# A message-passing kernel whose TensorE stages each lag the stage they need by one full step

## The chip, the core and the metric

The kernel runs on one core of a Trainium2 chip. The metric is device time in microseconds (us) of the whole program. The core's engines are TensorE (PE for its matmuls, PEld for its weight loads), VectorE (DVE), ScalarE (ACT), GpSimd (POOL) and SyncE (SP, which only issues DMAs here); they run at the same time and wait for one another through semaphores.

## The reference

A graph layer: 200,000 edges, sorted by their target node, over 12,500 nodes with 32 features each. Each edge goes through four dense layers, the results are averaged by target node, added to the node's features and normalised.

```python
x_j = x[j_idx]                       # source row
x_i = x[i_idx]                       # target row
msg = jnp.concatenate([x_i, x_j - x_i], axis=-1)   # 64
h = jax.nn.relu(msg @ W1 + b1)       # 64
h = jax.nn.relu(h @ W2 + b2)         # 128
h = jax.nn.relu(h @ W3 + b3)         # 64
m = h @ W4 + b4                      # 32
s = jax.ops.segment_sum(m, i_idx, num_segments=N_NODES)
cnt = jax.ops.segment_sum(jnp.ones((m.shape[0],), m.dtype), i_idx, num_segments=N_NODES)
...
x = _layernorm(x + s / jnp.maximum(cnt, 1.0)[:, None], axis=-1)
```

## The kernel before

**Steps.** The edges are worked on in 196 steps of 1,024 edges, two halves (h) of 512 each. Because the edges are sorted by target, a step touches only a narrow window of nodes, so the target's part of layer 1 and the sum by target are matmuls against small 0/1 matrices that VectorE builds (`build_pick`, L1259, L1260, L1262; `build_onehot`, L1301). The source rows come in one of two ways:

- **gathered steps** (138): GpSimd fetches rows already multiplied by W1 with 8 indirect DMAs of 128 rows each (L564) into a ring of ten steps, and TensorE turns them into layer 1's PSUM bank (`turn_rows`, L859). A slot of the ring is free again when its step has been turned, which is what GpSimd waits for.
- **sorted steps** (58): the edges of the step were sorted by source beforehand, and TensorE picks the rows by 113 small bf16 matmuls against one-hots (`selected_x`, L897). VectorE builds these one-hots in 8 chunks (`build_hot`, L1270) from index rows that SyncE spreads over all partitions (L467, 366 to 407 KB each); there are five buffers for them. ScalarE (L664) and VectorE (L1280) copy the picked rows to SBUF, and `selected_layer1` (L911) multiplies them by W1.

From step 14 on every third step is a sorted one, up to step 185: a **period** is one sorted and two gathered steps, and there are 58 of them. The first ten steps (AHEAD) run beside a sort on VectorE. Five of them are "plain": their rows are not yet multiplied by W1 (L872).

**Stages of a step.** Layer 1 with the target's part (`add_dst`, L841) → ReLU on ScalarE (L675) → layer 2 (L921) → ReLU (two halves, L683) → layer 3 (L929) → ReLU (L690) → turned (L937) → copied by VectorE (L1289) → summed by target window (L952, sorted steps L949) → added to the sums by VectorE (L1316). Each of the stages on TensorE has one PSUM buffer; the SBUF buffers between them are double.

**Order.** Every engine has an order written out by hand: a function `step(s)` per engine names what is done in round s, and for which step. TensorE's is, before the change: rows of s (for a sorted step all 113 matmuls), turn of s-2, window sum of s-3, the sorted step's layer 1, layer 3 of s-1, layer 2 of s. So layer 2 of s follows layer 1 of s in the same round, and layer 3 of s-1 stands one round after its layer 2. VectorE in round s builds chunks 5 to 7 of its one-hots if s is sorted, copies the rows, copies the turned layer 3 of s-2, builds the pick of s+1 and the one-hot of s-2, adds the sums of s-3, and builds chunks 0 to 4 for sorted steps ahead. An engine waits at its next instruction and everything behind it waits too.

## Time and profile before

| what | us |
|---|---|
| median of 3 runs | 2545.24 (2544.97 to 2545.98) |
| the profiled execution | 2551.01 |
| its span, first to last instruction | 2549.2 |
| TensorE matmul busy | 1782.1 (70%) |
| TensorE weight loads busy | 1173.7 (46%) |
| GpSimd busy | 1093.8 (43%) |
| VectorE busy | 844.8 (33%) |
| ScalarE busy | 634.2 (25%) |

The granted clock of TensorE over the span is 0.803 of full speed; it has two levels, 1.2 and 2.4 GHz. The table gives averages over a front part with a sort and few matmuls (to about 415 us), the 58 periods (to about 2415 us), a row of gathered steps and the last layer. In the profile a matmul's start is recorded and its end is modelled; when its result was really there is seen at the instruction of another engine that waited for it. "remote" as what ended a wait means that the profile finds no instruction whose recorded end fits it.

### The profile page before, as it was taken

The numbers are of one execution on the slowest core, as the hardware profiler recorded it, in microseconds if no ns is written. First come the engines' busy times: TensorE is split into PE (matmuls) and PEld (weight loads), VectorE is DVE, ScalarE is ACT, GpSimd is POOL, SyncE is SP. The second block draws the span as 40 slices with busy tenths as digits, with TensorE's granted clock in tenths as the row PEclk, the third lists the DMA queues.
The fourth block names the chain that finished last, engine by engine and source line by source line (L and its number), as shares of the span: only waits on it lengthen the run. The fifth ranks groups of instructions, "written<-read, shape, count | busy, mean of one in ns | idle before, by whom it ended". The sixth has DMA issues, their size and how long they took to land.

```text
span 2549.2 us, 39560 instructions
## 1 busy us (share of the span) xinstructions
PE 1782.1 (70%) x13928; PEld 1173.7 (46%) x13928; DVE 844.8 (33%) x1777; ACT 634.2 (25%) x999; POOL 1093.8 (43%) x1123
## 2 busy tenths in 40 slices
PE   2133516777787777787777777777877778777887
PEld 2111303555454554555554555554555545555547
DVE  2342602333333333333333333332333333333352
ACT  2222314222222222222222222222222222222241
POOL 4175263444444444444444444444344444444402
PEclk9975756878878788878888878888788888887885
DMA  3221414444434444444444444443444443444310
GB/s 114 81 65 29 114 35 149 142 133 133 132 112 140 137 139 125 126 123 142 139 138 125 127 123 142 136 138 105 128 142 137 139 123 120 131 142 133 93 58 27
DMA packets 194466, 300.61 MB, mean 118 GB/s; under 512 B 83633, under 2 KB 90015, under 8 KB 193697
## 3 DMA queue, kind: packets, MB, share of 16 engines
q1 hardware_dynamic: 158439, 260.74, 32.3%
q0 software_dynamic: 35168, 35.43, 6.7%
q8 instruction: 116, 1.90, 0.3%
q10 hardware_dynamic: 658, 1.85, 0.2%
q14 instruction: 85, 0.70, 0.1%
HBM read 283.89 MB, written 13.87 MB: 117 GB/s over the span
## 4 chain that ended last, share of the span: by engine, by line
PE 41%; another core or an unknown queue 22%; issue 16%; DVE 9%; DMA 5%; ACT 3%; DVEq 3%; SPq 0%; POOL 0%; ACTq 0%; POOLq 0%
PE ps L897 21%; PE ps L921 5%; PE ps L929 3%; PE ps L949 3%; DVEq L1314 3%; PE ps L937 2%; PE ps L841 2%; PE ps L911 2%; PE ps L998 2%; DVE region L1270 2%; DVE region L1301 2%; PE ps L859 1%; DMA dstb<-dst_rows 1%; DMA y_rows<-work 1%
## 5 line engine op out<-in xcount | busy, mean ns | idle before, releaser
L564 POOL DMA_INDIRECT xj<-z_rows,src_t x1059 | 1038.2, 980 | 1293.4 <-PE ps L859 785.6
L897 PE MATMUL ps<-region,x_p 128*96 128x155 bf16 (+51 forms) x6554 | 611.4, 259 | 268.5 <-issue 238.0
L897 PEld LDWEIGHTS ps<-region,x_p 128*96 128x96 bf16 x6554 | 544.1, 162 | 395.4 <-issue 367.3
L1270 DVE TENSOR_SCALAR region<-region,cst 128x1629 bf16<-128x1629 int16 x464 | 274.0, 643 | 348.6 <-remote 295.1
L929 PE MATMUL ps<-work,w3s 128*64 128x512 f32 x784 | 311.5, 697 | 69.0 <-ACT work L683 38.5
L683 ACT ACTIVATE work<-ps,b2s 128x512 f32<-128x512 f32 x392 | 256.8, 685 | 205.7 <-remote 147.0
L1289 DVE COPY work<-ps 128x512 f32<-128x512 f32 x188 | 129.2, 687 | 504.0 <-remote 278.5
L921 PE MATMUL ps<-work,w2s 64*128 64x512 f32 x784 | 252.9, 726 | 45.5 <-ACT work L675 41.1
L690 ACT ACTIVATE work<-ps,b3s 128x512 f32<-128x512 f32 x196 | 134.7, 687 | 529.6 <-remote 468.4
L675 ACT ACTIVATE work<-ps,b1s 128x512 f32<-128x512 f32 x196 | 134.8, 688 | 507.7 <-PE ps L841 363.0
L937 PE MATMUL ps<-cst,work 128*128 128x128 f32 x784 | 138.3, 303 | 139.8 <-ACT work L690 99.3
L1316 DVE TENSOR_TENSOR sums<-sums,ps 65x42 f32 (+1 forms) x334 | 67.7, 203 | 361.3 <-remote 179.0
L952 PE MATMUL ps<-region,work 128*65 128x42 f32 x2208 | 177.3, 248 | 12.4 <-issue 6.6
L952 PEld LDWEIGHTS ps<-region,work 128*65 128x65 f32 x2208 | 175.8, 159 | 12.9 <-issue 11.5
L921 PEld LDWEIGHTS ps<-work,w2s 64*128 64x128 f32 x784 | 65.4, 204 | 237.0 <-ACT work L675 164.8
L937 PEld LDWEIGHTS ps<-cst,work 128*128 128x128 f32 x784 | 89.7, 150 | 178.0 <-ACT work L690 112.4
L664 ACT ACTIVATE work<-ps 96x512 bf16<-96x512 f32 x58 | 34.4, 593 | 491.5 <-PE ps L897 491.5
L929 PEld LDWEIGHTS ps<-work,w3s 128*64 128x64 f32 x784 | 61.4, 150 | 150.4 <-ACT work L683 84.4
L1280 DVE CAST work<-ps 96x512 bf16<-96x512 f32 x58 | 39.8, 687 | 247.5 <-PE ps L897 247.5
L859 PEld LDWEIGHTS ps<-cst,xj 128*128 128x128 f32 x552 | 59.8, 144 | 127.5 <-issue 127.5
L859 PE MATMUL ps<-cst,xj 128*128 128x128 f32 x552 | 93.6, 294 | 20.5 <-DVE work L1233 19.3
L841 PE MATMUL ps<-region,ywin 126*64 126x512 bf16 x508 | 93.1, 400 | 20.8 <-DVE region L1262 11.6
(156 smaller groups left out, 940.2 us busy)
## 6 DMA issues: line engine op xcount, KB each, us to landing
dstb<-dst_rows SPq DMA_DIRECT2D x196, 252.0 KB
region<-src_rows SPq DMA_DIRECT2D x116, 391.2 KB
region<-src_rows SPq DMA_DIRECT2D x58, 407.2 KB
region<-src_rows SPq DMA_DIRECT2D x58, 403.2 KB, 4.8
region<-src_rows SPq DMA_DIRECT2D x58, 376.2 KB
region<-src_rows SPq DMA_DIRECT2D x58, 375.8 KB, 3.7
region<-src_rows SPq DMA_DIRECT2D x58, 374.0 KB
region<-src_rows SPq DMA_DIRECT2D x58, 366.2 KB, 5.4
```

Source lines behind the costliest of these rows:

```text
L564: pool.indirect_dma_start(out=xj[:, u, j % UT, j // UT, 0:w], out_offset=None, in_=rows, in_offset=bass.IndirectOffsetOnAxis(ap=cols[:, j: ...
L675: nc.scalar.activation(h1[:, v, :], p_h1, ACT.Relu, bias=b1s[:, 0:1]).then_inc(s_r1, 1)
L683: nc.scalar.activation(h2[:, v, h, :], p_h2[:, h, :], ACT.Relu, bias=b2s[:, 0:1]).then_inc(s_r2[h], 1)
L690: nc.scalar.activation(h3[:, v, :], p_h3, ACT.Relu, bias=b3s[:, 0:1]).then_inc(s_r3, 1)
L841: added = nc.tensor.matmul(p_h1[h * H1:(h + 1) * H1, :], rows, pick[:, v, k, h * UE:(h + 1) * UE], start=False, stop=k == steps - 1, skip_ ...
L859: turned = nc.tensor.matmul(to[:, t * T:(t + 1) * T], xj[:, u, t, :, :].rearrange("p h f -> p (h f)"), ident, start=t == 0, stop=True, is_ ...
L897: chosen = nc.tensor.matmul(ps[0:XP, XBANK[h], lo - h * UE:hi - h * UE], xb[:, a, :], hot[:, q % QN, at + lo:at + hi], start=not begun[h], ...
L921: nc.tensor.matmul(p_h2[:, h, :], w2s[r:r + H1, :], h1[r:r + H1, s % 2, :], start=True, stop=True).then_inc(s_l2[h], 1)
L929: nc.tensor.matmul(p_h3[h * H3:(h + 1) * H3, :], w3s[:, :], h2[:, s % 2, h, :], start=True, stop=True).then_inc(s_l3, 1)
L937: turned = nc.tensor.transpose(p_ht[:, t * T:(t + 1) * T], h3[:, s % 2, t * T:(t + 1) * T], ident)
L952: summed = nc.tensor.matmul(p_agg[:, h * KN:(h + 1) * KN], h3t[:, v, t, h, :], onehot[:, v, j, 0:KN], start=t == 0, stop=t == UT - 1)
L1270: nc.vector.tensor_scalar(hot[:, q % QN, 0:CW[c]], spread[:, q % QE, 0:CW[c]], cst[:, C_PID:C_PID + 1], None, ALU.is_equal).then_inc(s_hot, 1)
```

## The change

TensorE's round s becomes: layer 1 of s (for a sorted step it needs the rows already picked), then **the picking of rows for s+1 if that one is sorted**, layer 2 of s-1, layer 3 of s-2, turn of s-3, window sum of s-4. Each stage now needs what was done a full round earlier. ScalarE and VectorE follow in the same manner: the ReLUs of a round come in the order 1, 2, 3 for s, s-1, s-2; the copies of the picked rows are for s+1; VectorE first adds the sums of s-5, and the one-hot chunks come a step earlier than before (chunks 0 and 1 three steps ahead, 2 to 4 two, 5 to 7 one). The first sorted step is 15 instead of 14, so one more gathered step stands ahead of the periods and one fewer behind them, and each engine has one round more to empty the pipeline. SyncE's loads of index rows move a round earlier as well. GpSimd's code is untouched.

```diff
-FIRST_SORTED, PERIOD = AHEAD + 4, 3
+FIRST_SORTED, PERIOD = AHEAD + 5, 3
...
             def step(s):
-                if is_sorted(s) and STEPS[s] + 1 < SB:
+                if s + 1 < S_N and is_sorted(s + 1) and STEPS[s + 1] + 1 < SB:
                     for c in range(CN - QN):
-                        load_windows(STEPS[s] + 1, QN + c)
+                        load_windows(STEPS[s + 1] + 1, QN + c)
                 if s + RX < S_N:
                     load_dst(s + RX)
                     load_rows(s + RX)
...
-                if s + 1 < S_N and is_sorted(s + 1) and STEPS[s + 1] + 1 < SB:
+                if s + 2 < S_N and is_sorted(s + 2) and STEPS[s + 2] + 1 < SB:
                     for c in range(QN):
-                        load_windows(STEPS[s + 1] + 1, c)
+                        load_windows(STEPS[s + 2] + 1, c)
...
             def step(s):
-                if s >= 1:
-                    relu2(s - 1)
-                if s < S_N and is_sorted(s):
-                    copy_x(s)
                 if s < S_N:
                     relu1(s)
-                if 2 <= s < AHEAD:
-                    copy_layer3(s - 2)
-                if s >= 1:
-                    relu3(s - 1)
+                if s + 1 < S_N and is_sorted(s + 1):
+                    copy_x(s + 1)
+                if 1 <= s <= S_N:
+                    relu2(s - 1)
+                if 2 <= s <= S_N + 1:
+                    relu3(s - 2)
+                if 3 <= s < AHEAD:
+                    copy_layer3(s - 3)
...
             def step(s):
+
                 if s < S_N:
                     if is_sorted(s):
-                        selected_x(s)
+                        selected_layer1(s)
                     elif is_plain(s):
                         plain_x(s)
                     else:
                         gathered_x(s)
+                if s + 1 < S_N and is_sorted(s + 1):
+                    selected_x(s + 1)
+                if 1 <= s <= S_N:
+                    layer2(s - 1)
                 if 2 <= s <= S_N + 1:
-                    turn_layer3(s - 2)
-                if s >= 3:
-                    sum_window(s - 3)
-                if s < S_N and is_sorted(s):
-                    selected_layer1(s)
-                if 1 <= s <= S_N:
-                    layer3(s - 1)
-                if s < S_N:
-                    layer2(s)
+                    layer3(s - 2)
+                if 3 <= s <= S_N + 2:
+                    turn_layer3(s - 3)
+                if s >= 4:
+                    sum_window(s - 4)
...
             def step(s):
-                if s < S_N and is_sorted(s):
+                if s >= 5:
+                    add_sums(s - 5)
+                if s + 1 < S_N and is_sorted(s + 1):
                     for c in range(QN, CN):
-                        build_hot(STEPS[s], c)
-                if s < S_N and (is_sorted(s) or is_plain(s)):
+                        build_hot(STEPS[s + 1], c)
+                    copy_x(s + 1)
+                if s < S_N and is_plain(s):
                     copy_x(s)
-                if AHEAD <= s <= S_N + 1:
-                    copy_layer3(s - 2)
                 if s + 1 < S_N:
                     build_pick(s + 1)
-                if 2 <= s <= S_N + 1:
-                    build_onehot(s - 2)
-                if s >= 3:
-                    add_sums(s - 3)
-                for lead, some in ((2, (0, 1)), (1, (2, 3, 4))):
+                if AHEAD <= s <= S_N + 2:
+                    copy_layer3(s - 3)
+                if 3 <= s <= S_N + 2:
+                    build_onehot(s - 3)
+                for lead, some in ((3, (0, 1)), (2, (2, 3, 4))):
```

The order on TensorE, before, from the second gathered step of a period to the first matmuls that pick the sorted step's rows (L897), with the semaphores each row waits for (`relu2_unit0` and `relu2_unit1` are ScalarE's two halves):

```order
L859 MATMUL ps<-cst,xj 128x128 [waits gathered1,relu1]
L859 MATMUL ps<-cst,xj 128x128 x3
L841 MATMUL ps<-region,ywin 64x512 [waits pick_built,window_in1]
L841 MATMUL ps<-region,ywin 64x512
L937 MATMUL ps<-cst,work 128x128 [waits layer3_copied,relu3]
L937 MATMUL ps<-cst,work 128x128 x3
L952 MATMUL ps<-region,work 65x42 [waits sums_added,onehot_built,layer3_copied]
L952 MATMUL ps<-region,work 65x42 x7
L929 MATMUL ps<-work,w3s 64x512 [waits relu2_unit0,relu3]
L929 MATMUL ps<-work,w3s 64x512 [waits relu2_unit1]
L921 MATMUL ps<-work,w2s 128x512 [waits relu2_unit0,relu1]
L921 MATMUL ps<-work,w2s 128x512 [waits relu2_unit1]
```

And now, in the same place; a line number of the changed kernel is that of before plus one here:

```order
L860 MATMUL ps<-cst,xj 128x128 [waits gathered4,relu1]
L860 MATMUL ps<-cst,xj 128x128 x3
L842 MATMUL ps<-region,ywin 64x512 [waits pick_built,window_in2]
L842 MATMUL ps<-region,ywin 64x512
L898 MATMUL ps<-region,x_p 96x26 [waits source_onehots,x_copied_unit1,x_copied_unit0]
...
L898 MATMUL ps<-region,x_p 96x20
L922 MATMUL ps<-work,w2s 128x512 [waits relu2_unit0,relu1]
L922 MATMUL ps<-work,w2s 128x512 [waits relu2_unit1]
L930 MATMUL ps<-work,w3s 64x512 [waits relu2_unit0,relu3]
L930 MATMUL ps<-work,w3s 64x512 [waits relu2_unit1]
```

The picking (all its rows lie at the "...") moved from behind the whole second gathered step to right behind its layer 1; the four stages that stood ahead of it now follow it, and they are of older steps.

On VectorE, before, the round of a sorted step: chunks 5 to 7 of the one-hots (`chunks_selected` tells that TensorE is done with an older chunk) stand ahead of the copies and the pick.

```order
L1270 TENSOR_SCALAR region<-region,cst 128x1503
L1270 TENSOR_SCALAR region<-region,cst 128x1613
L1270 TENSOR_SCALAR region<-region,cst 128x1465
L1280 CAST work<-ps 96x512
L1289 COPY work<-ps 128x8x64
L1262 TENSOR_SCALAR region<-dstb,node_off 126x1024
L1301 TENSOR_TENSOR region<-iota_g,dst_rel 128x8x42
```

Now this stands in the round of the gathered step ahead of it, behind that round's sums:

```order
L1318 TENSOR_TENSOR sums<-sums,ps 65x84
L1272 TENSOR_SCALAR region<-region,cst 128x1503
L1272 TENSOR_SCALAR region<-region,cst 128x1613
L1272 TENSOR_SCALAR region<-region,cst 128x1465
L1282 CAST work<-ps 96x512
L1261 TENSOR_SCALAR region<-dstb,node_off 126x1024
L1262 TENSOR_SCALAR region<-dstb,node_off 126x1024
L1291 COPY work<-ps 128x8x64
```

The sums moved to the head of the round, and the copy of the turned layer 3 moved behind the pick.

## Rows read from the trace of the kernel before

**Rows 1.** The page: part 1 (busy, share); of part 5 one group (busy, mean | idle before).

```profile
PE 1782.1 (70%) x13928; PEld 1173.7 (46%) x13928; DVE 844.8 (33%) x1777; ACT 634.2 (25%) x999; POOL 1093.8 (43%) x1123
...
L897 PE MATMUL ps<-region,x_p 128*96 128x155 bf16 (+51 forms) x6554 | 611.4, 259 | 268.5 <-issue 238.0
```

**Rows 2.** Table by stretch: front part with two gather stretches, then the periods.

```profile
core 0: us, PE busy (x) PEld busy (x) DVE busy (x) ACT busy (x) POOL busy (x), PEclk, DMA share, GB/s
...
130.00:243.00 113.00, 30.23 (x88) 11.75 (x88) 39.34 (x93) 21.96 (x22) 79.89 (x79) 0.63 0.23 50
...
302.00:381.00 79.00, 17.52 (x81) 9.32 (x79) 5.71 (x11) 16.46 (x46) 53.20 (x56) 0.54 0.19 41
...
415.00:2415.00 2000.00, 1551.00 (x12590) 1024.63 (x12591) 669.50 (x1382) 485.02 (x742) 888.91 (x907) 0.82 0.44 132
```

**Rows 3.** Timeline of TensorE in a gathered step while GpSimd is idle.

```profile
2424.69 0.66 PE L859 MATMUL ps<-cst,xj 128*128 128x128 f32 x4
...
2425.61 0.66 PE L937 MATMUL ps<-cst,work 128*128 128x128 f32 x4
...
2429.19 0.66 PE L859 MATMUL ps<-cst,xj 128*128 128x128 f32 x4
```

**Rows 4.** Table by stretch of one period, in its order; the last is another block.

```profile
1515.16:1519.66 4.50, 4.50 (x36) 2.48 (x35) 1.50 (x3) 1.85 (x3) 2.84 (x3) 1.00 0.34 87
1519.66:1530.68 11.02, 8.55 (x36) 3.27 (x34) 3.93 (x8) 2.75 (x4) 7.38 (x8) 0.69 0.25 48
1530.68:1539.32 8.64, 3.84 (x45) 3.07 (x44) 2.21 (x5) 1.84 (x3) 5.46 (x6) 0.89 0.84 250
1539.32:1545.36 6.04, 6.04 (x70) 6.04 (x71) 1.67 (x3) 0.59 (x1) 0.00 (x0) 0.59 0.70 214
1545.36:1550.30 4.94, 4.94 (x43) 2.72 (x41) 2.34 (x5) 1.38 (x2) 0.00 (x0) 1.00 0.18 47
...
2407.70:2415.27 7.57, 6.70 (x116) 6.38 (x114) 4.17 (x9) 2.44 (x4) 1.58 (x2) 1.00 0.24 51
```

**Rows 5.** Timeline of TensorE in the two gathered steps of that period.

```profile
1517.59 1.08 PE L929 MATMUL ps<-work,w3s 128*64 128x512 f32 x4
...
1519.66 0.66 PE L859 MATMUL ps<-cst,xj 128*128 128x128 f32 x4
...
1522.56 0.66 PE L937 MATMUL ps<-cst,work 128*128 128x128 f32 x4 [1.91 <-ACT work L690]
...
1524.31 1.97 PE L929 MATMUL ps<-work,w3s 128*64 128x512 f32 x2
1526.84 1.97 PE L929 MATMUL ps<-work,w3s 128*64 128x512 f32 x2 [0.56 <-ACT work L683]
1528.74 2.02 PE L921 MATMUL ps<-work,w2s 64*128 64x512 f32 x4
```

**Rows 6.** Timeline of GpSimd: first gather of a period, ninth, sixteenth, next period's first.

```profile
1516.09 0.94 POOL L564 DMA_INDIRECT xj<-z_rows,src_t  x1 [14.12 <-PE ps L859]
...
1527.77 0.95 POOL L564 DMA_INDIRECT xj<-z_rows,src_t  x1 [1.64 <-remote]
...
1536.73 0.94 POOL L564 DMA_INDIRECT xj<-z_rows,src_t  x1 [0.30 <-issue]
1551.20 0.95 POOL L564 DMA_INDIRECT xj<-z_rows,src_t  x1 [13.53 <-PE ps L859]
```

**Rows 7.** Timelines of ScalarE and VectorE: instructions that waited for TensorE's results.

```profile
1521.82 0.69 ACT L690 ACTIVATE work<-ps,b3s 128x512 f32<-128x512 f32 x1 [4.72 <-remote]
...
1526.10 0.69 ACT L683 ACTIVATE work<-ps,b2s 128x512 f32<-128x512 f32 x1 [2.14 <-remote]
```

**Rows 8.** Timeline of TensorE: the picking of rows while GpSimd gathers.

```profile
1530.68 1.75 PE L897 MATMUL ps<-region,x_p 128*96 128x26 bf16 x29
1533.10 0.75 PE L897 MATMUL ps<-region,x_p 128*96 128x146 bf16 x5 [0.66 <-DVE region L1270]
```

**Rows 9.** Waits of the front part (130 to 415 us): in total, times, longest.

```profile
ACT work L690 <- remote: 45.9, 3, 27.4
```

More of the change, by code:

```diff
@@ L357, in layer3_copied @@
         def layer3_copied(eng, s):
-            if s < AHEAD - 2:
+            if s < AHEAD - 3:
                 eng.wait_ge(s_h3a, s + 1)
             else:
-                eng.wait_ge(s_h3c, s + 3 - AHEAD)
+                eng.wait_ge(s_h3c, s + 4 - AHEAD)
         def piece(h):
@@ L726, in _ @@
                     nc.scalar.activation(src16[:, :], scr0.bitcast(I32), ACT.Copy).then_inc(s_cast, 1)
+            act.wait_ge(s_cast, 2)
             act.wait_ge(s_end, 1)
@@ L729, in _ @@
             with act.Fori(0, end, WIN) as off:
-                for s in range(AHEAD, S_N + 1):
+                for s in range(AHEAD, S_N + 2):
                     step(s)
-                    if AHEAD <= s < SSTEP[0] - 1:
+                    if AHEAD <= s < SSTEP[0] - 2:
                         for c in range(3 * (s - AHEAD), min(3 * (s - AHEAD) + 3, CN)):
@@ L986, in _ @@
             with pe.Fori(0, end, WIN) as off:
-                for s in range(AHEAD, S_N + 3):
+                for s in range(AHEAD, S_N + 4):
                     step(s)
@@ L1369, in _ @@
                 mask_sorted()
-                for s in range(AHEAD, S_N + 3):
+                for s in range(AHEAD, S_N + 5):
                     step(s)
```

6 lines of the change are left out of this document (3 added, 3 removed).

## Prediction, made before the changed kernel ran

> **What bounds the kernel now.** I read the share of each engine first. TensorE's matmuls are busy 70% of the span and GpSimd's gathers 43% [rows 1], so TensorE is the bound, with 30% in which it stands. The table by stretch says where the time lies: 2,000 of the 2,549 us are the 58 periods; the front part has two long stretches, 113 and 79 us, in which TensorE has only 88 and 81 matmul records [rows 2].
>
> Next, a step that nothing disturbs. With GpSimd idle a gathered step takes 2429.19 - 2424.69 = 4.50 us, one group of matmuls right behind the other, no wait [rows 3]. There the old order hides every round trip already: a deeper pipeline could give nothing.
>
> Then one period by its stages [rows 4]: first gathered step 4.50, second gathered step 11.02, picking of rows 8.64 + 6.04, rest of the sorted step 4.94; together 35.1 us. The second gathered step and the picking are the slow ones: undisturbed they take 4.50 [rows 3] and 7.57, the last row of [rows 4]. What the slow parts share is GpSimd: its 16 gathers run from 1516.09 to 1537.67, with one pause of 1.64 us, and it is idle until 1551.20 [rows 6]. Inside that stretch two things are seen.
>
> First, TensorE's results are told late. The first gathered step's layer 3 is issued at 1517.59 and should be done a us later, yet its ReLU on ScalarE starts at 1521.82, after 4.72 us without an instruction; a half of layer 2's ReLU starts 1526.10, for a layer 2 that stands ahead of the turn at 1519.66 [rows 5, 7]. So a round trip costs 3 to 7 us instead of one. TensorE then waits itself: 1.91 us for the ReLU of layer 3, and layer 3's halves, which ran side by side in 1.08 us a step earlier, are issued 2.53 us apart and take 1.97 us each, at the lower clock (granted mean 0.69) [rows 4, 5].
>
> Second, small instructions crawl although nothing they wait for is missing. Picking starts with 29 matmuls in 1.75 us [rows 8]; up to 1539.32 there are 43 (the 45 records of that stretch less two of the layer 2 ahead), so the last 14 take 1539.32 - 1533.10 = 6.2 us, 2.3 a us; behind it come 70 in 6.04 us, 11.6 a us [rows 4]. The end of the crawl is 1.65 us behind the last gather's end.
>
> **The change part by part.** No matmul, DMA, copy or activation of a period is added or removed; it is a matter of order.
>
> (a) *Second gathered step.* Its layer 1 (L859, L841) takes 0.92 us, turn, sum, layer 3 and layer 2 the other 3.58 [rows 3]. All four now need what was done a round earlier, so the round trips of 3 to 7 us lie under a round of 4.5. The parts of the two gathered steps that stay inside the gather stretch are 3.58 + 0.92 = 4.5 us of work instead of 15.5 - 0.9 = 14.6 us of time. Gain at most 14.6 - 4.5 = 10.1 us, of which 3.58 is only moved behind the picking.
>
> (b) *Picking moves into the crawl.* It begins about 4.5 to 5.5 us into the gather stretch instead of 14.6, so about 9 us more of it meet the crawl. TensorE's period, counted from the first gather, is then: end of the crawl at 1539.32 - 1516.09 = 23.2; what is left of the 113 matmuls at 0.086 us each (6.04 / 70); 3.58 for the four stages behind them; 4.94 for the sorted step; 0.9 to the turn that frees GpSimd. That is 32.6 + 0.086 x (113 - k), k being the matmuls issued by the end of the crawl. The old order fits the same sum: 23.2 + 6.04 + 4.94 + 0.9 = 35.1. For k: at the crawl's slow rate 43 + 9 x 2.3 = 64, period 36.8; all 113, period 32.6; at the mean rate of the old 8.64 us (5.0 a us) 43 + 9 x 5.0 = 88, period 34.8. I take 88: the picking now also has the early, livelier part of the stretch and GpSimd's pause, where the old order had only the end. Gain 0.3 us x 58 = 17 us.
>
> (c) *VectorE and ScalarE.* VectorE's work of a period (11.7 us by its rows [rows 4]) is the same. Chunks 5 to 7 of the one-hots now wait for TensorE a round earlier, with the copy of the picked rows, the two picks and the copy of layer 3 queued behind; who needs them is the next round's layer 1 and turn, 3.58 us of TensorE's work later. The picks and copies take about 2.4 us, so this is hidden; if that cover goes, it costs up to 1 us a period. ScalarE's copy of the picked half stands ahead of the ReLU of layer 2, whose matmul comes behind the picking anyway: nothing. SyncE's index rows move a round earlier, and the loads of target rows three steps ahead are queued behind them as before: nothing. GpSimd's gathers are freed by the same turn.
>
> (d) *Front part.* In the two gather stretches TensorE issues a matmul each 113 / 88 = 1.3 us and 79 / 81 = 1.0 us [rows 2], and one ReLU of layer 3 waits 27.4 us [rows 9]. The new order puts off layer 2, layer 3, turn and sum of a step by a round: about 20 to 28 records that lie ahead of the next rows in the crawl and are later paid at 4.5 us a step. Ends: a gain of 28 x 1.3 - 4.5 = 32 us, or no gain (below zero too: a loss of 5, if GpSimd's gathers are freed sooner and the crawl lasts longer). I take 20, since VectorE, too, no longer waits for sums of s-3 but of s-5.
>
> (e) *End.* One more round to empty the pipeline, one gathered step fewer behind the periods; the same matmuls. Between 0 and one step of 4.5 us; I take 2.
>
> Sum against the profiled execution: 2551.0 - 17 - 20 + 2 = 2516; the median of the runs shown is 5.8 us below that execution, so 2510.
>
> **A rule that speaks against my reading.** The rows show matmuls slow while GpSimd gathers and fast once it stops [rows 4, 6, 8]. The Trainium skill, "SBUF — State Buffer", section "SBUF: two separate sides", says that TensorE's SBUF port never waits for anyone and that only VectorE and GpSimd share a port. By it the gathers would cost TensorE nothing; the trace so far speaks against it, and the rival built on it is the last one below.
>
> **Rivals.**
>
> *Slower: the picking crawls all the way.* It decides from k: 35.1 = 32.6 + 0.086 x (113 - k) gives k = 84, that is 4.6 matmuls a us over the added 9 us; with the front's gain of 20 us (0.34 a period) the even point is k = 80. At 2.3 a us the period is 36.8: +1.7 x 58 = +99, with -20 and +2 about 2626. For it: 14 matmuls in 6.2 us are the only direct sample of that rate, and in the front part, where gathers run without a pause for longer, the rate is 1 a us. Now nothing stops GpSimd for 1.64 us if the second turn is told sooner. Against it: 29 matmuls went through at full pace, and the change gives TensorE the stretch's beginning.
>
> *Much faster: nothing of the picking is left when the gathers end.* k = 113, period 32.6: -2.5 x 58 = -145, with -20 about 2382. For it: 17.7 us are there for work that takes 7.57 undisturbed. Against it: chunk 5's one-hots need the first chunk reported as done, and this is just what comes late.
>
> *No change.* The stretch lets a fixed amount of work through whatever its order, and the front gains nothing: 2545. For it: the stretch's end hangs on GpSimd alone in both orders.
>
> *GpSimd disturbs nothing; the slow parts are round trips only.* Then the period falls to 4.5 + 4.5 + 7.6 to 10 + 4.9, about 22.5 us, still over GpSimd's 16 gathers, (1537.67 - 1516.09 - 1.64) = 19.9 us [rows 6]: -12.6 x 58, about 1800. Against it: 238.0 of the 268.5 us that TensorE idles ahead of the picking's matmuls end with no wait at all [rows 1].
>
> **How the numbers follow.** Forecast as summed, 0.40, with a range of its own of 2470 to 2535; slower 0.33; much faster 0.12; no change 0.12; the last rival 0.03. A range that leaves out no more than two in ten reaches from the much faster case to most of the slower one: 2380 to 2612. What a measurement of this kernel can tell from no change is about 0.2%, 5 us. Faster: 0.40 + 0.12 + 0.03 = 0.55; same 0.12; slower 0.33.
>
> **What would show each step right or wrong.** (a): in the gather stretch, no wait of layers 2 and 3 or of the turn for ScalarE; two gathered steps' worth of work ahead of the picking in about 5 us. (b): count the picking's matmuls between its start and the end of the crawl, and the period from one first gather to the next: below 35.1 or above. (c): a wait of layer 1 of the sorted step for a pick or a copied half would be new. (d): the periods begin at about 415 us [rows 2], and one gathered step more stands ahead of them now; a first picking that starts ahead of 415 shows the gain. The prediction falls if the picking's rate in the stretch is below 4 a us, or if GpSimd's pause, and so the stretch, becomes longer.

## The result, and the profile after

The changed kernel took 2684.82 us (median of 4 runs, 2681.97 to 2688.92), the kernel before beside it 2545.17 (4 runs): a ratio of 1.0549, 95% interval 1.0531 to 1.0568. It is 5.5% slower. The forecast was 2510 with a range of 2380 to 2612, so both the sign and the range were wrong. The profiled execution spans 2683.2 us.

The page of the changed kernel, shares of the engines and the groups that answer to [rows 1]. Line numbers of TensorE's code are higher by one now (picking is L898), those of VectorE by two:

```profile
PE 1691.2 (63%) x13928; PEld 1144.3 (43%) x13928; DVE 839.3 (31%) x1778; ACT 613.6 (23%) x998; POOL 1090.5 (41%) x1123
...
L898 PE MATMUL ps<-region,x_p 128*96 128x155 bf16 (+51 forms) x6554 | 677.1, 259 | 678.9 <-issue 678.6
...
L1272 DVE TENSOR_SCALAR region<-region,cst 128x1629 bf16<-128x1629 int16 x464 | 275.7, 637 | 896.9 <-remote 827.8
...
L930 PE MATMUL ps<-work,w3s 128*64 128x512 f32 x784 | 215.5, 627 | 0.5 <-ACT work L690 0.5
```

TensorE is busy for 63% instead of 70%. Its idle time ahead of picking matmuls rose from 268.5 to 678.9 us, nearly all of it "issue": time in which it waited for nothing that the profile shows. Its waits for ScalarE's ReLUs are gone: 0.5 us ahead of layer 3 in the whole span. In the kernel before they were 38.5 us there, 41.1 ahead of layer 2 and 99.3 ahead of the turn, the largest (total, times, longest):

```profile
PE ps L937 <- ACT work L690: 99.3, 39, 15.1
```

So the lag did what it says, and the time is lost elsewhere.

Where it is lost, from the timeline of TensorE in the changed kernel: the start of the first picking, of the second and of the last.

```profile
405.30 1.50 PE L898 MATMUL ps<-region,x_p 128*96 128x26 bf16 x15
...
435.13 0.80 PE L898 MATMUL ps<-region,x_p 128*96 128x26 bf16 x13
...
2536.39 1.31 PE L898 MATMUL ps<-region,x_p 128*96 128x26 bf16 x22
```

In the kernel before these stood at 414.92, 446.65 and 2407.70. The part up to the second picking is 11.5 us shorter; the 56 periods behind it take (2536.39 - 435.13) / 56 = 37.52 us instead of 35.02, which is +140 us; the rest of the span, 146.8 us instead of 141.5, is +5.3. The three make +134, the difference of the two spans.

One period of the changed kernel, in its order, as [rows 4] shows one of before: the work between the first gather and the picking, the early part of the picking, its crawl, its rest, and all up to the next period's first gather.

```profile
core 0: us, PE busy (x) PEld busy (x) DVE busy (x) ACT busy (x) POOL busy (x), PEclk, DMA share, GB/s
...
1593.06:1597.65 4.59, 4.59 (x37) 2.62 (x35) 3.47 (x9) 2.53 (x4) 3.67 (x4) 1.00 0.26 59
1597.65:1600.37 2.72, 1.68 (x30) 1.56 (x28) 1.24 (x3) 0.00 (x0) 2.11 (x3) 1.00 0.74 220
1600.37:1616.07 15.70, 4.24 (x28) 2.99 (x27) 0.62 (x1) 0.69 (x1) 9.91 (x11) 0.60 0.43 133
1616.07:1621.51 5.44, 5.44 (x61) 5.42 (x61) 1.15 (x2) 0.59 (x1) 0.00 (x0) 0.59 0.49 187
1621.51:1630.60 9.09, 9.09 (x73) 4.78 (x73) 5.03 (x11) 4.37 (x7) 0.00 (x0) 1.00 0.22 65
```

Work goes at full pace for 4.59 us of gathers, then the picking puts through 27 matmuls and crawls for 15.70 us, in which only 27 more are issued: 1.7 a us. The crawl's inside, from the timeline of TensorE:

```profile
1597.65 1.69 PE L898 MATMUL ps<-region,x_p 128*96 128x26 bf16 x27
1600.37 0.29 PE L898 MATMUL ps<-region,x_p 128*96 128x143 bf16 x2 [1.04 <-issue]
1601.12 0.23 PE L898 MATMUL ps<-region,x_p 128*96 128x146 bf16 x1 [0.46 <-issue]
...
1611.79 0.44 PE L898 MATMUL ps<-region,x_p 128*96 128x124 bf16 x3 [2.37 <-issue]
1614.62 0.38 PE L898 MATMUL ps<-region,x_p 128*96 128x44 bf16 x3 [2.39 <-issue]
1615.36 0.31 PE L898 MATMUL ps<-region,x_p 128*96 128x93 bf16 x1 [0.35 <-issue]
1616.07 5.44 PE L898 MATMUL ps<-region,x_p 128*96 128x65 bf16 x59 [0.40 <-issue]
```

Matmuls come out one to four at a time, with 0.30 to 2.39 us between, and each gap is "issue". GpSimd's timeline, as in [rows 6]: first gather of the period, ninth, sixteenth, the next period's first.

```profile
1593.06 1.21 POOL L564 DMA_INDIRECT xj<-z_rows,src_t  x1 [17.28 <-PE ps L860]
...
1603.57 0.94 POOL L564 DMA_INDIRECT xj<-z_rows,src_t  x1 [0.30 <-issue]
...
1612.30 1.03 POOL L564 DMA_INDIRECT xj<-z_rows,src_t  x1 [0.30 <-issue]
1630.60 1.21 POOL L564 DMA_INDIRECT xj<-z_rows,src_t  x1 [17.27 <-PE ps L860]
```

The pause of 1.64 us ahead of the ninth gather [rows 6] is gone. That holds for the whole trace: in the kernel before the break lasts 1.2 to 2.05 us in every period, here it is the 0.30 us that lie between any two gathers. The sixteen run in one unbroken row, most starts 1.25 us apart (mean 1.28), and the crawl ends 2.7 us behind the last of them. The clock adds to it. TensorE stands for most of the crawl (4.24 us busy of 15.70), its granted clock falls to a mean of 0.60, and the 59 matmuls behind take 5.44 us at a mean of 0.59: the lower of its two levels, 0.50, up to 1620.0, the upper one at the end; a whole picking of 113 takes 6.4 us at full clock (below).

### The profile page after: what moved, and what is told of

Read it like the earlier page. It is cut to its first block, busy times and chain, and to the rows that moved or that the text cites. A ratio compares the mean times of both kernels' runs of the same rounds, so it can differ in the third digit from the quotient of the medians.

```text
span 2683.2 us, 39558 instructions
## 1 busy us (share of the span) xinstructions
PE 1691.2 (63%) x13928; PEld 1144.3 (43%) x13928; DVE 839.3 (31%) x1778; ACT 613.6 (23%) x998; POOL 1090.5 (41%) x1123
## 3 DMA queue, kind: packets, MB, share of 16 engines
q0 software_dynamic: 35168, 35.43, 6.3%
## 4 chain that ended last, share of the span: by engine, by line
PE 57%; issue 26%; DMA 1%; DVE 1%; DVEq 0%; POOL 0%; SPq 0%; ACT 0%; POOLq 0%
PE ps L898 25%; PE ps L922 7%; PE ps L930 7%; PE ps L953 4%; PE ps L938 4%; PE ps L950 3%; PE ps L842 2%; PE ps L860 2%; PE ps L912 2%; PE ps L1000 2%; DMA region<-in_x 1%; DVEq L1316 0%; DMA src_rows<-region 0%; DMA region<-src_rows 0%; POOL region L596 0%
## 5 line engine op out<-in xcount | busy, mean ns | idle before, releaser
L898 PE MATMUL ps<-region,x_p 128*96 128x155 bf16 (+51 forms) x6554 | 677.1, 259 | 678.9 <-issue 678.6
L898 PEld LDWEIGHTS ps<-region,x_p 128*96 128x96 bf16 x6554 | 570.2, 159 | 793.8 <-issue 790.2
L1272 DVE TENSOR_SCALAR region<-region,cst 128x1629 bf16<-128x1629 int16 x464 | 275.7, 637 | 896.9 <-remote 827.8
L683 ACT ACTIVATE work<-ps,b2s 128x512 f32<-128x512 f32 x392 | 248.5, 684 | 316.4 <-PE ps L922 287.3
L922 PE MATMUL ps<-work,w2s 64*128 64x512 f32 x784 | 234.2, 670 | 6.2 <-issue 6.2
L930 PE MATMUL ps<-work,w3s 128*64 128x512 f32 x784 | 215.5, 627 | 0.5 <-ACT work L690 0.5
L953 PE MATMUL ps<-region,work 128*65 128x42 f32 x2208 | 155.8, 233 | 74.5 <-DVE sums L1318 38.8
L953 PEld LDWEIGHTS ps<-region,work 128*65 128x65 f32 x2208 | 152.8, 143 | 75.6 <-issue 74.4
L938 PE MATMUL ps<-cst,work 128*128 128x128 f32 x784 | 129.6, 287 | 2.1 <-issue 2.0
L930 PEld LDWEIGHTS ps<-work,w3s 128*64 128x64 f32 x784 | 39.6, 136 | 156.6 <-issue 154.7
L950 PE MATMUL ps<-region,work 128*65 128x84 f32 x928 | 77.9, 238 | 7.7 <-DVE sums L1318 7.7
```

Of the source, the lines that this page charges most:

```text
L683: nc.scalar.activation(h2[:, v, h, :], p_h2[:, h, :], ACT.Relu, bias=b2s[:, 0:1]).then_inc(s_r2[h], 1)
L898: chosen = nc.tensor.matmul(ps[0:XP, XBANK[h], lo - h * UE:hi - h * UE], xb[:, a, :], hot[:, q % QN, at + lo:at + hi], start=not begun[h], ...
L922: nc.tensor.matmul(p_h2[:, h, :], w2s[r:r + H1, :], h1[r:r + H1, s % 2, :], start=True, stop=True).then_inc(s_l2[h], 1)
L930: nc.tensor.matmul(p_h3[h * H3:(h + 1) * H3, :], w3s[:, :], h2[:, s % 2, h, :], start=True, stop=True).then_inc(s_l3, 1)
L938: turned = nc.tensor.transpose(p_ht[:, t * T:(t + 1) * T], h3[:, s % 2, t * T:(t + 1) * T], ident)
L950: summed = nc.tensor.matmul(p_agg, h3t[:, v, t, h, :], onehot[:, v, j, :], start=j == 0, stop=j == PT - 1)
```

## The experiments

The eighteen runs fell on six chips, A to F. The kernel before ran on each, and **it finds two kinds of chip**. On A, C and D it took 2546.8, 2570.0 and 2559.4 us, much as on the chip of the result; on B, E and F 1608.8, 1611.1 and 1613.7 us. I call them the first and the second kind; nothing in a program chooses one. Each chip was used for one short time only, so whether the kind belongs to the chip for good or to its state at the time is not shown. Each run is told against the kernel before on its own chip; on A to D each time is that of a single run. Periods are mean distances between the starts of pickings, the second to the last, as above.

**One gather instead of eight, old order and new** (chip A, first kind; before 2546.8 us). The other rows of each step are left out of the computation; the sums are those of wrong rows.

```
 def gathers_of(g):
+    if g >= AHEAD + 5:
+        return 1
     return PT if g < GB - 1 else LAST
```

> The kernel before with 1 of the 8 row gathers of each gathered step from the 16th gathered step on (the other rows stay stale; sums are those of wrong rows). Theory D (GpSimd's gathers make TensorE's small instructions crawl and its results late): the period falls from 35.0 us to about 4.5 + 4.5 + 7.6 to 10 + 4.9 = 22 to 24 us, total about 2545 - 57 x 12 = 1860. Theory R (the slow parts of the period are round trips and waits of TensorE, ScalarE and VectorE among themselves): nothing changes, 2540. Theory L (the loads of index rows, 3.1 MB a period, make it crawl): nothing changes, 2540.

> The changed kernel with the same gathers left out. Theory D: 22 to 24 us a period as in the kernel before, within 1 us of it, total 1840 to 1880; what the new order costs is gone. Theory W (the new order has a wait of its own, for one-hot chunks or index rows that now come too late): still 2.5 us a period slower than the kernel before without gathers, about 140 us in all.

Measured: 1661.13 us for the old order, 1644.87 for the new, periods of 20.24 and 20.14 us. That is theory D in kind, and some 200 us below its numbers, which had put the period at 22 to 24 us. The table by stretch of the new order with one gather, over 1,100 us of its periods:

```profile
360.00:1460.00 1100.00, 1100.00 (x11976) 757.11 (x11975) 612.74 (x1314) 447.91 (x711) 129.66 (x110) 1.00 0.62 205
```

TensorE is busy all the time at full clock. So 15 to 17 us of each period go with the gathers, in either order. Without them the new order is 16 us the faster, so it holds no wait of its own, and the index-row loads of SyncE, which are all still there, cost nothing by themselves. The change loses only where the gathers are; whether they need the loads beside them to do harm is not shown, since no run leaves the loads out.

**Gathers put behind the picking** (chip A).

```
 if g >= R:
     pool.wait_ge(s_turned, g - R + 1)
+if g >= AHEAD + 5:
+    picked = sum(1 for s in SSTEP if s < GSTEP[g - R]) + 1
+    if GSTEP[g - R] > SSTEP[0] and picked <= SB:
+        pool.wait_ge(s_block, CN * picked)
```

> The changed kernel with one wait more: in the periods GpSimd starts a step's gathers only when TensorE has finished the picking that follows (the chunks_selected semaphore). The 16 gathers (19.9 us) then start beside layers 2 and 3 of the second gathered step and lie on 13.9 us of large matmuls before they meet the next picking. Theory D: at most 6 us of gathers plus 2.7 us behind them fall on the picking; period about 29 us, total 2685 - 57 x 8 = about 2230, below both kernels. Theory W: no gain, 2685 or more; theory that GpSimd's gathers are needed early: a new wait of TensorE for gathered rows.

A miss, and the most useful one: 2683.2 us, period 37.46. The picking now runs at full pace, as no gather lies beside it, and what gets slow is the work that lies beside the gathers instead. TensorE's timeline in that kernel:

```profile
1505.56 1.01 PE L926 MATMUL ps<-work,w2s 64*128 64x512 f32 x1 [1.55 <-issue]
1507.66 1.01 PE L926 MATMUL ps<-work,w2s 64*128 64x512 f32 x1 [1.09 <-issue]
1510.48 1.86 PE L926 MATMUL ps<-work,w2s 64*128 64x512 f32 x2 [1.82 <-issue]
...
1519.14 6.45 PE L902 MATMUL ps<-region,x_p 128*96 128x26 bf16 x113
```

Layer 2, four matmuls in 1.13 us when nothing disturbs them, takes from 1505.56 to 1512.3 (the granted clock is 0.50 there). So the loss belongs to the row of gathers and not to the kind of work beside it: my picture of a picking that "crawls" and of larger steps that mostly wait for round trips was too narrow. A period of 37.5 us is not far from 20.1 us of work and 20 us of gathers one after the other, here and in the changed kernel.

**The lag alone, picking in its own round** (chip A). Of the diff, the later stages keep their full step of lag; the picking, its copies, one-hots and loads go back to the step that uses them.

```
 def step(s):
     if s < S_N:
         if is_sorted(s):
-            selected_layer1(s)
+            selected_x(s)
 ...
-    if s + 1 < S_N and is_sorted(s + 1):
-        selected_x(s + 1)
 ...
+    if s < S_N and is_sorted(s):
+        selected_layer1(s)
```

> The change without its second half: each stage lags by a full step, but the rows of a sorted step are picked in its own round, ahead of layer 2 of the step before, and layer 1 of the sorted step closes the round; first sorted step 14 as before. Theory D: the picking begins 3.6 us later in the gather stretch than in the changed kernel, so of the crawl at 1.7 matmuls a us it loses 6 matmuls (0.5 us) and gains 3.6 us of large matmuls: period 37.5 - 3.1 = 34.4, total about 2500. If the deeper lag itself costs: about 2685 as the changed kernel.

Measured: 2589.78 us, period 35.83, a miss too (2500 and 34.4 were expected). The lag alone costs 43 us, and the picking ahead of its step another 95 (against the 2684.82 us of the result's chip; the changed kernel as it is did not run on A): neither pays. In this kernel GpSimd still pauses for some 2 us between the eighth and the ninth gather of a period; with the picking ahead the pause is gone. That is the lead that the run with one pause follows, below. Why the lag alone makes the period 0.8 us longer than the 35.02 of before was not followed up.

**Room between the gathers** (chips B and C). Two theories were left. N: each gather costs about 1 us wherever it lies. B: what costs is the unbroken row, and gathers with room between them are free. Behind each gather from the sixteenth gathered step on, GpSimd writes a small tile of its own and waits for that write. Nothing is left out of the computation.

```
     pool.indirect_dma_start(out=xj[:, u, j % UT, j // UT, 0:w], ...)
         .then_inc(s_gath[u], 16)
+    if g >= AHEAD + 5:
+        nc.gpsimd.memset(pause[:, :], 0.0).then_inc(s_pause, 1)
+        paused[0] += 1
+        pool.wait_ge(s_pause, paused[0])
```

> The changed kernel, with a small write of GpSimd's own (one partition, 192 values) and a wait for it behind every gather from the sixteenth gathered step on: the gathers stay 16 a period, but their starts are some 1.7 to 1.9 us apart instead of 1.25. Theory B (what slows TensorE is the unbroken row of gathers, and single ones with room between cost nothing): the crawl goes or shrinks, the period falls from 37.5 to about 28 to 32 us (16 gathers then take 28 to 30), some 2150 to 2400 us. Theory N (each gather costs about 1 us wherever it lies; 20.2 us of work + 16 x 1.08): the period stays at 37.5 and the time within 1% of 2684.

> The same with 768 values in GpSimd's write, so that the gathers start some 2.2 to 2.6 us apart. Theory B: TensorE no longer waits for anything but the gathers themselves, 16 x 2.2 to 2.6 = 35 to 41 us a period, GpSimd busy throughout, the picking at its full pace of 6.4 us; 2550 to 2900 us. Theory N: the sum of both, the gathers' loss of 1.08 us each on 20.2 us of work while the gathers take 35 to 41, so the picking and the other steps still lose about 17 us a period; the time is then at least 2684.

> The changed kernel with 4 of the 8 gathers of each gathered step from the sixteenth on (the other rows keep what the buffer held: this part of the computation is left out), 8 a period instead of 16. Theory N (a loss for each gather): the period is 20.2 + 8 x 1.08 = 28.8 us, about 2190 us. Theory B (nothing below four or five gathers in a row, then a crawl): bursts of 4 with room between, a period of 20.2 to 22 us, 1640 to 1760 us; where the two bursts of 4 join to one of 8, about 24 us and 1900.

Chip B is of the second kind, with the kernel before at 1608.83 us. Short pause 1860.72 us (period 24.7), long pause 2315.97 us (32.3), four gathers of eight 1561.94 us (20.14). There was no crawl to take away, so these say nothing on what the crawl hangs on. They say what a pause costs: GpSimd becomes the bound.

> The changed kernel as it is, on whichever chip this call gets. The runs so far fell on two chips: on the first the kernel before took 2545 to 2547 us, on the second 1608.8, with all that the gathers cost on the first gone. On a chip of the first kind: 2684 us, 5.5% above before. On one of the second kind there is no crawl to lose by, and both theories leave TensorE as the bound: period 20.2 us as in the runs with one gather, so 1580 to 1600 us, 1 to 2% below before, from the hidden round trips alone.

> The kernel of e6_pause_short again. On a chip of the second kind 1861 us as there. On one of the first kind it tells what the first call was meant to: theory B (the unbroken row is what slows TensorE): with starts 1.54 us apart the crawl shrinks and the period falls to 25 to 32 us, 1900 to 2400 us; theory N (a loss of 1.08 us for each gather wherever it lies): the period stays at 37.5 us, some 2684.

> The changed kernel with one pause of some 1.5 to 2 us of GpSimd between the eight gathers that the first gathered step of a period releases and the eight of the second (a write of 1300 values on one partition and the wait for it). On a chip of the first kind: if the unbroken row of 16 is what the change costs in a period (37.5 against 35.0 us), the period falls to about 35 us, 2540 to 2560 us; if the break is worth nothing, 37.5 us and 2684; if the pause only adds, 38 to 39. On one of the second kind: the 16 gathers take 20 us of a period of 20.2, so the pause makes GpSimd the bound at about 22 us, 1680 to 1710 us.

Chip C is of the first kind, before at 2569.98 us. The changed kernel took 2679.41 us (period 37.51): slower again, here by 4.3%. With the short pause it took **1957.47 us**, 27% less, and 24% less than the kernel before, with the same gathers and the same work; period 25.6. GpSimd's timeline in it:

```profile
863.93 0.95 POOL L568 DMA_INDIRECT xj<-z_rows,src_t  x1 [0.27 <-issue]
864.88 0.25 POOL L572 MEMSET pause<- 1x192 f32 x1
865.40 0.95 POOL L568 DMA_INDIRECT xj<-z_rows,src_t  x1 [0.27 <-issue]
```

Starts are 1.47 us apart instead of 1.25 (a mean of 1.6, where some of the writes take longer), and 16 x 1.6 = 25.6 us is the period: the gathers' own time is the bound now. TensorE beside it, in one of the periods with a remnant of the crawl:

```profile
859.99 5.00 PE L906 MATMUL ps<-region,x_p 128*96 128x26 bf16 x84
865.29 0.31 PE L906 MATMUL ps<-region,x_p 128*96 128x144 bf16 x2 [0.29 <-issue]
866.00 0.47 PE L906 MATMUL ps<-region,x_p 128*96 128x141 bf16 x5 [0.40 <-issue]
866.75 0.37 PE L906 MATMUL ps<-region,x_p 128*96 128x132 bf16 x3 [0.28 <-issue]
```

84 matmuls go through at full pace while GpSimd gathers. Theory N, a fixed cost for each gather wherever it lies, has fallen: by it the period would have stayed at 37.5 us. Theory B holds: gathers with room between them do little harm. One thing it leaves open: the room was always made by a write of GpSimd's and a wait for it, so that the write or the wait itself, and not only the distance, does the good is a rival that no run excludes.

One longer pause between the eighth and the ninth gather, the tile written only there (`if g >= AHEAD + 5 and j == PT - 1 and GSTEP[g - R + 1] == GSTEP[g - R] + 1`, 1300 values of bf16; 1600 found no room in SBUF), gives 2568.79 us and a period of 35.81, against 2569.98 for the kernel before and 2679.41 without it (expected were 2540 to 2560 us and about 35). GpSimd's timeline there:

```profile
1131.91 0.94 POOL L568 DMA_INDIRECT xj<-z_rows,src_t  x1 [0.30 <-issue]
1132.85 1.17 POOL L572 MEMSET pause<- 1x1300 bf16 x1
1134.29 0.95 POOL L568 DMA_INDIRECT xj<-z_rows,src_t  x1 [0.27 <-issue]
```

GpSimd stands for 1.44 us there, as for the 1.64 of before [rows 6]. Of the 110.6 us gained, (37.51 - 35.81) x 56 = 95 lie in the periods, the rest up to the second picking. And 35.81 is the period of the kernel with the lag alone (35.83, on chip A), which has such a pause by itself. So what the picking ahead of its step cost the periods, (37.52 - 35.83) x 56 = 95 us, is as much as the lost pause cost on chip C, and no part is seen that would need another cause. A wait that looked like a flaw, GpSimd told late of the second turn, had kept the period down. It is not the whole story: 35.81 is still 0.8 us above the 35.02 of before, at a granted clock of 0.75 over the periods (450 to 1500 us) where the kernel before has 0.82. The total is level with before because the periods begin sooner, the first picking at 376.81 us.

**Old order with the pause, the shortest pause, and all gathers paused** (chip D, first kind; before 2559.35 us). The edits are that of the short pause on the kernel before; the same with a tile of one value; and the same without its condition, so that the front part's gathers are paused too.

> The kernel before with the short pause of GpSimd (a write of 192 values and the wait for it) behind every gather from the sixteenth gathered step on. On a chip where the crawl exists: theory B (the rate of the gathers in a row decides, 1.25 us apart is too close and 1.6 is nearly wide enough) gives the period that 16 x 1.6 = 25.6 us of gathers set, as in the changed kernel with the same pause, plus what GpSimd waits for the later second turn (1.6 us): 26 to 28 us, 1960 to 2080 us against 1957 of the changed kernel. If instead the new order is needed for the gain, the period stays near 35 us, 2500. On a chip without crawl: 1850 to 1950 us, slower than the kernel before.

> The changed kernel with the shortest such pause, a write of a single value, so that the gathers start about 1.40 us apart: 16 take 22.4 us. If 1.40 us is wide enough, the gathers set a period of 22.5 to 23.5 us and the time is 1780 to 1840 us; if the limit lies between 1.40 and 1.60 us, the crawl is back in part: a period of 28 to 34 us, 2100 to 2450 us. Theory N (a cost per gather) has fallen with e10.

> The changed kernel with the pause of 192 values behind every gather, those of the first 15 gathered steps too. On a chip where the crawl exists the front part then loses it as well: the first picking starts at 260 to 300 us instead of 347 us (e10), the period stays 25.6, so 1870 to 1910 us. If the front part is slowed by something else (its own loads), the first picking stays at about 347 us or later, 1957 us or more. On a chip without crawl: 1861 us or up to 20 us more.

Old order with the pause: 1942.52 us, period 24.5, both a little below what was expected. The new order is not needed for the gain; with both paused they are within 1%, on two chips. The shortest pause: 2393.06 us, period 32.5. In most of a row its starts are 1.31 us apart, where 1.40 was expected (the mean is 1.43, since some writes and waits take longer in the crawl):

```profile
1111.13 0.94 POOL L568 DMA_INDIRECT xj<-z_rows,src_t  x1 [0.27 <-issue]
1112.08 0.09 POOL L572 MEMSET pause<- 1x1 f32 x1
1112.43 0.94 POOL L568 DMA_INDIRECT xj<-z_rows,src_t  x1 [0.27 <-issue]
```

So the period falls from 37.5 us at 1.25 us between starts (mean 1.28) to 32.5 at 1.31 (mean 1.43) and 25.6 at 1.47 (mean 1.6), where the gathers themselves are the bound. Everything paused: 1885.10 us, and the first picking starts at 261.93 us instead of the 347.22 of the short pause, which leaves the gathers of the first 15 gathered steps as they are:

```profile
261.93 1.81 PE L906 MATMUL ps<-region,x_p 128*96 128x26 bf16 x18
```

Those gathers had cost 85 us. Against the changed kernel with no pause at all (399.75 us on chip C, 405.30 in the result) the front part had lost some 140 us, and what is left of it is as short as on the second kind, where the changed kernel's first picking starts at 263.93 us.

**The paused old order, and the changed kernel where there is no crawl** (chips E and F, second kind; before 1611.14 us in 7 runs, and 1613.74 in 3). The first edit is the pause of 192 values behind every gather of the kernel before, the second that of 128 values.

> The kernel before with the pause of 192 values behind every gather, the front part's too. The paused kernels so far: 1942.5 us for the order of before with a slow front part (period 24.5), 1885.1 us for the new order with a quick one (period 25.8). If the pause's two gains add, the front part's 85 us (first picking at 262 to 275 us instead of 352) come off 1942.5: 1855 to 1875 us, under both kernels and under the paused new order. If not, 1885 to 1945 us. On a chip without crawl: 1850 to 1870 us, slower than the kernel before there.

> The same with 128 values, so that gathers start some 1.45 to 1.50 us apart. If the limit lies below that, the gathers' period of 16 x 1.47 = 23.5 us is seen: about 1800 us. If it lies between 1.47 and 1.6 us, the crawl returns in part of the periods: 1900 to 2200 us (1.40 us apart the period was 32.5).

> The changed kernel as it is. Where the gathers slow TensorE: 2680 us, 5% over the kernel before. On a chip where they don't: the period is TensorE's 20.2 us in both, and the new order gains the front part and the ends of its rounds as in the kernels with one gather (1661 to 1645): 1585 to 1600 us, 0.5 to 1.5% under the kernel before.

> The kernel of e15 again, which on the chip without crawl took 1871.5 us. Its GpSimd is the bound there, so on a chip of the other kind (the kernel before at 2545 to 2570 us) the same 1855 to 1890 us, 27% under the kernel before; if the front part stays slow, up to 1945 us.

> The kernel of e16 again, 1830 us on the chip without crawl. On the other kind: 1830 to 1850 us if gathers about 1.5 us apart are far enough from each other; with the limit above that, 1900 to 2200 us.

Measured: 1871.50 us with 192 values (4 runs; 1871.39 on F in 2), 1830.36 with 128 (4 runs; 1830.14 on F in 2): 16% and 14% slower than the kernel before there (on E 1.160 to 1.165, and 1.132 to 1.140). Both chips are of the second kind, so what these two give on the first stays open; the nearest there are the 1885.10 and 1942.52 us of chip D. The changed kernel took 1578.61 us (2 runs on E) against 1611.14: **a ratio of 0.980, interval 0.978 to 0.983, about 2% faster on this kind of chip**, a little more than the 0.5 to 1.5% expected. Its table by stretch over the periods:

```profile
285.00:1385.00 1100.00, 1100.00 (x11986) 757.14 (x11984) 636.74 (x1312) 445.59 (x708) 842.48 (x846) 1.00 0.74 228
```

and its two engines in one period, TensorE and then GpSimd:

```profile
668.20 6.44 PE L898 MATMUL ps<-region,x_p 128*96 128x26 bf16 x113
```

```profile
671.12 1.02 POOL L564 DMA_INDIRECT xj<-z_rows,src_t  x1 [0.30 <-issue]
672.45 0.94 POOL L564 DMA_INDIRECT xj<-z_rows,src_t  x1 [0.30 <-issue]
673.70 0.94 POOL L564 DMA_INDIRECT xj<-z_rows,src_t  x1 [0.30 <-issue]
```

All 113 matmuls of a picking go through in 6.44 us while gathers of the same 0.94 us start every 1.25 us. TensorE is busy 100% of 1,100 us; the period is 20.14.

## Why the prediction was wrong, by its steps

(a) *Second gathered step*: right. The work between the first gather and the picking takes 4.59 us, TensorE is busy for all of them, and so no round trip stops it there. As forecast, the picking starts some 4.5 us into the stretch.

(b) *Picking moves into the crawl*: this is the step that failed, in one term, k, the matmuls issued by the end of the crawl. The sum itself held: 32.6 + 0.086 x (113 - k) with the measured k = 27 + 27 = 54 gives 37.7 us, and 37.52 was measured. In its 23.2 us for the end of the crawl there is some luck: 23.0 were measured, but the last gather ended 1.3 us sooner without the pause, and the crawl ended 2.7 us behind it instead of 1.65. What was wrong is k = 88, at 5.0 matmuls a us over the added 9 us. The rate was 1.7 a us over 15.70 us, below even the 2.3 that I had as the slow end. The old stretch's mean was no sample of the rate deep in a row of gathers: its 8.64 us began with 29 matmuls at full pace, 2.9 us behind the end of GpSimd's pause. The slow bound was measured behind that pause too. The rival "the picking crawls all the way" had the mechanism and the sign; its 2626 us was short because 2.3 a us was still too fast (period 36.8 instead of 37.52) and its gain in the front part too large.

The second error in this step is what I said of the pause itself: that nothing would stop GpSimd any more stood in the rival, as a remark without a price. The run with one pause put back gives the price: 95 us in the periods, 111 in all, and with it the changed kernel is level with the kernel before (2568.79 and 2569.98 us). With that price the forecast would have been slower, not faster. The remark in (c), "GpSimd's gathers are freed by the same turn", was true and missed this: the same turn is told at least 1.6 us sooner relative to the gathers ahead of it.

(c) *VectorE, ScalarE, SyncE*: nothing, as forecast. VectorE waits much more ahead of the one-hots (896.9 us idle). The profile names no releaser for most of it ("remote"); that it waits for the reports of the crawling picking is argued. With one gather the new order has TensorE busy 100% of the time, so none of its waits is on the path.

(d) *Front part*: a gain of 9.6 us to the first picking and 11.5 to the second, of 20 forecast and within the ends of 32 and -5. The paused runs show what was really there to be had: some 140 us.

(e) *End*: +5.3 us instead of +2, and over its upper end of 4.5. Some 2.7 us of (d)'s gain and of this loss are the same work counted elsewhere: at its first picking the new order has done one layer 1 more (0.92 us) and the four later stages once less (3.58 us).

The sum with the measured terms: +140 for the periods, -11.5 and +5.3, is +134 us; with 2551.0 us for the profiled execution before that is 2685.

"GpSimd disturbs nothing" had 0.03, and on three of the six chips it is true. There the changed kernel's 1578.6 us is even below that rival's 1800, since its period was put at 22.5 us and is 20.14, and since the front part is 141 us shorter too. The forecast was made from one trace, and that trace holds a property of its chip that another chip of the same type did not show. On the rule weighed in the prediction, of the Trainium skill, "SBUF — State Buffer", section "SBUF: two separate sides", that TensorE's port waits for no one: a TensorE that is busy 100% beside unbroken gathers agrees with it. The crawl of the first kind goes against what the prediction made of it, that gathers cost TensorE nothing; no run here shows that the crawl has to do with SBUF's ports at all, so the rule itself is not refuted.

**What stays open.** What in the first kind of chip holds up TensorE's instructions, and the telling of its results to ScalarE, while gathers come every 1.25 us. (In the period shown the ReLU of layer 1 starts at 1602.00, behind matmuls issued at 1597.31.) The gathers' issue is alike on both (0.94 us each, 1.25 apart), and so is the time that their packets take. The rows are of the gathers' queue in the page, for the changed kernel on the first kind (span 2683.2 us) and on the second (1576.7):

```profile
q0 software_dynamic: 35168, 35.43, 6.3%
```

```profile
q0 software_dynamic: 35168, 35.43, 10.1%
```

6.3% of 2683 is 169 us for each of the 16 engines, 10.1% of 1577 is 159 us: nearly the same. That the crawl begins some four to seven gathers into a row, ends 1.5 to 3 us behind it, and all but goes when starts are 1.47 us apart looks like something that is served more slowly than each 1.25 us and backs up, but no run shows what. The Trainium skill, "Perfetto Trace Analysis", section "DMA Instruction — SWDGE (GPSIMD)", says that such an instruction's end in the profile is the end of writing its descriptors and not of the movement; if so, a backlog would not be seen in GpSimd's rows, and none is. The trace agrees with the page: a gather's instruction takes 0.94 us, and its packets run from 1.65 us behind its start on.

The movement can be looked at by itself, and it is not what backs up. A gather is 32 packets of that queue (35168 packets for 1099 gathers), in order. For the ninth to the fifteenth gather of a row in the changed kernel, deep in the crawl, the first packet starts 1.65 us behind the gather's start and the last ends 2.1 us behind it (medians over the periods), one like the other. On the second kind, where nothing crawls, they are later: 3.4 and 4.4 us. Nor are the DMA engines full. In the middle of the crawl shown above their busy share is 0.13, at 26 GB/s, while TensorE has 4 matmuls in 3.75 us; on the second kind TensorE is busy all the time beside a share of 0.74.

```profile
1607.30:1611.05 3.75, 0.72 (x4) 0.47 (x4) 0.00 (x0) 0.00 (x0) 2.83 (x3) 0.50 0.13 26
```

Whether the instructions themselves come late is not shown: the queues that the page calls "instruction" move the same 201 packets on both kinds, and a packet of the larger of them takes 1.0 to 1.1 us beside gathers on either, but the trace does not tell when one was asked for.

Where the 32 us of gain on the second kind come from was not traced in the kernel before there; with one gather the two orders differ by 16 us, 10 of it ahead of the first picking.

## What to carry to other kernels

Before moving work beside a row of transfers, sample the rate at the depth of the row (how many transfers have gone ahead without a break) where the work will lie, and price any break in it that the change removes: the wait that spaced the transfers may be what kept the rest moving. Where small gathers from GpSimd come back to back and other engines show idle time that ends in "issue", try a short pause between them: against the kernel before it was worth 24 to 26% on one kind of chip, and cost 14 to 16% on the other. So run the kernel before on more than one chip ahead of such a choice: the sign of this change, about -2% or +4.3 to +5.5%, goes with it.

## What the runs showed of the hardware

- Chips of the same type differ by a factor of 1.6 on one program: 2546.8, 2570.0, 2559.4 us on three, 1608.8, 1611.1, 1613.7 us on three others, within 0.4% on a chip where it ran more than once. With one gather in eight in the periods the first kind reaches 1661.13, so nearly the whole gap hangs on the gathers. No chip was seen at two times, so whether it keeps its kind is open.
- On the first kind, in a row of 16 gathers 1.25 us apart and the 2.7 us behind it, 23 us in all, TensorE gets through work that takes 4.6 + 54/113 x 6.44 = 7.7 us undisturbed; at 1.31 us (mean over a row 1.43) the period falls from 37.5 to 32.5 us, at 1.47 (mean 1.6) to 25.6, GpSimd's own time. Single gathers with room around them cost nothing (period 20.14 us with two).
- The crawl hits whatever lies beside the gathers: picking matmuls, layer 2 (6.8 us instead of 1.13), and the front part (first picking at 261.93 us with all gathers paused, at 399.75 and 405.30 with none).
- It is not the gathers' own movement: deep in the crawl a gather's packets are done 2.1 us behind its start, sooner than the 4.4 us on the second kind, and the DMA engines' busy share in the middle of the crawl shown is 0.13.
- The clock makes it dearer: TensorE's granted clock fell to a mean of 0.60 in a stretch in which it was busy 4.24 of 15.70 us, and the next 5.44 us ran at a mean of 0.59; a picking of 113 takes 6.44 us at 1.00, so 59 of them would take 3.4: 2.0 us a period. The old order pays as much (70 in 6.04 us [rows 4]), so this part explains none of the difference between the two, only some of what both lose to the gathers.
